# VectorE adds x for every group of the experts; layer norm of attended values on 33 rows a batch; eight unread products a batch

## The reference, cut to what matters

```python
# layer 3: of the 512 tokens of a batch 32 are chosen by score, the others get -1e9
scores = jnp.full_like(scores, -1000000000.0).at[b_idx, topk_idx].set(topk_vals)
return jax.nn.sigmoid(scores)         # their gate is 0, and all of them have one attended row
...
x = x + _layernorm(_L1_attn_ref(_layernorm(x, axis=-1), ...), axis=-1)

# layer 4: a causal attention, and then 8 experts, 2 of them chosen for a token
for e in range(N_EXPERTS):
    out = out + comb[:, e, None] * (t @ expert_w[e].T)
...
out = h + _moe(_rmsnorm(h, ffn_norm_w), gate_w, expert_w)
...
x = x + _layernorm(_L1_ffn_ref(_layernorm(x, axis=-1), ...), axis=-1)

def _layernorm(x, axis=-1, eps=1e-05):
    m = jnp.mean(x, axis=axis, keepdims=True)
    v = jnp.var(x, axis=axis, keepdims=True)
    return (x - m) / jnp.sqrt(v + eps)
```

## Time and profile before

| | us |
|---|---|
| median of 3 runs | 673.86 (671.64 to 676.05) |
| profiled execution, time | 673.91 |
| profiled execution, span | 672.2 |
| busy: PE / DVE / ACT / POOL | 552.9 / 505.7 / 360.5 / 269.6 |
| mean granted clock of PE | 0.848 of full |

### The profile page before, as it was taken

One profiled execution on the slowest core, in us unless ns is written; L12 is line 12 of the kernel. 1 busy time (PEld: TensorE's weight loads), 2 busy tenths in 40 slices (PEclk: granted clock), 3 DMA queues, 4 the chain that ended last, 5 costly groups with the idle time before them and its releaser, 6 DMA issues. The chain is left out here.

```text
span 672.2 us, 11846 instructions
## 1 busy us (share of the span) xinstructions
PE 552.9 (82%) x3809; PEld 313.0 (47%) x3809; DVE 505.7 (75%) x2306; ACT 360.5 (54%) x738; POOL 269.6 (40%) x501
## 2 busy tenths in 40 slices
PE   1875567988867999777999999999999898999870
PEld 1875467986656666311233333333333455465330
DVE  6599999454383778788899999999998056379784
ACT  5841134610200567501588788788878765466762
POOL 2001007721002476700354454545455454366784
PEclk9986675557967789855599999999999898999996
DMA  8000000210000066310011111111210000000001
GB/s 316 2 1 1 0 1 32 78 42 8 1 1 1 10 200 203 118 59 7 0 43 52 40 31 36 37 32 38 58 39 1 7 1 1 2 0 16 33 16 62
DMA packets 18876, 27.33 MB, mean 41 GB/s; under 512 B 3230, under 2 KB 14126, under 8 KB 18638
## 3 DMA queue, kind: packets, MB, share of 16 engines
q1 hardware_dynamic: 18174, 24.34, 11.6%
q10 hardware_dynamic: 576, 2.10, 0.9%
q0 software_dynamic: 64, 0.13, 0.1%
HBM read 14.11 MB, written 12.45 MB: 40 GB/s over the span
## 5 line engine op out<-in xcount | busy, mean ns | idle before, releaser
L904 DVE CUSTOM_DVE_ANT_0 w_qkvT<-d_pS,w_qkvT 128x512 bf16<-128x512 f32 x480 | 203.9, 485 | 17.3 <-PE d_pS L895 12.5
L1576 ACT ACTIVATE d_P<-pT 128x768 f32<-128x768 f32 (+1 forms) x192 | 165.9, 882 | 63.7 <-PE pT L1602 62.2
L1456 POOL TENSOR_SCALAR_AFFINE_SELECT d_P<-d_P 128x256 f32<-128x256 f32 x256 | 102.7, 415 | 134.7 <-ACT d_P L1576 134.7
L895 PE MATMUL d_pS<-Ks,Qs 48*128 48x512 bf16 x480 | 98.0, 325 | 13.3 <-DVE hadamard L904 8.9
L1602 PE MATMUL d_pO<-d_P,V 128*32 128x512 f32 (+3 forms) x1024 | 99.3, 463 | 1.4 <-POOL d_P L1456 0.9
L1602 PE MATMUL pT<-Qs,Ks 51*128 51x512 bf16 (+3 forms) x512 | 72.6, 311 | 1.9 <-ACT d_mT L1546 1.9
L895 PEld LDWEIGHTS d_pS<-Ks,Qs 48*128 48x128 bf16 x480 | 32.2, 96 | 56.7 <-DVE hadamard L904 52.0
L1602 PEld LDWEIGHTS pT<-Qs,Ks 51*128 51x128 bf16 x512 | 20.7, 94 | 73.8 <-ACT d_P L1576 42.8
L904 DVE DVE_READ_ACCUMULATOR2_ANT hadamard<- 128x1 f32 x512 | 42.5, 83 | 0.0
L1602 PEld LDWEIGHTS d_pO<-d_P,V 128*32 128x32 f32 x1024 | 21.3, 110 | 32.5 <-issue 29.6
L446 POOL MEMSET a_expS<- 1x1024 f32 x4 | 3.8, 945 | 78.7 <-DVE a_q L257 78.7
(11 more groups left out here) (314 smaller groups left out, 1073.1 us busy)
## 6 DMA issues: line engine op xcount, KB each, us to landing
Qs<-q_stack SPq DMA_DIRECT2D x32, 192.0 KB, 3.0
q_stack<-Qp SPq DMA_DIRECT2D x8, 384.0 KB, 2.5
X<-in_x_dram ACTq DMA_DIRECT2D x4, 512.0 KB, 6.2
n_rows<-N SPq DMA_DIRECT2D x4, 512.0 KB, 2.8
q_stack<-Qp SPq DMA_DIRECT2D x8, 256.0 KB, 2.5
out_dram<-e_moe SPq DMA_DIRECT2D x8, 256.0 KB, 2.0
w_qkvT<-in_w_qkvT_dram SPq DMA_DIRECT2D x1, 1536.0 KB
Ks<-k_stack SPq DMA_DIRECT2D x32, 48.0 KB, 3.2
```

Of the source, the lines that this page charges most:

```text
L895: last = nc.tensor.matmul(dst[:, at:at + w], top.Qs[c][rows, h % 8, 128 * q:128 * q + 128], top.Ks[c][rows, h // 4 % 2, 0:w], start=True, ...
L904: last = nc.vector.tensor_tensor_reduce(out=junk[:, at:at + w], in0=src[:, at:at + w], in1=top.wide_mask[:, 512 - w:512], scale=1.0, scala ...
L1456: last = nc.gpsimd.affine_select(out=view, in_=view, compare_op=ALU.is_ge, fill=0.0, base=0, pattern=[[0, 2], [1, 128]], channel_multiplie ...
L1576: nc.scalar.activation(P[pair % 4][:, :, P_AT[unit]:P_AT[unit] + w], pT[(3 * pair + unit) % 2][:, :, 0:w], ACT.Exp, scale=float(HD4) ** -0 ...
```

## The change

Projections: the norm of the attended values is taken ahead of the turns, on the rows themselves: for each half of the batches (Q), the 32 full rows a batch and the shared row, `Y + yU` and `yU`, get moments, a root, and are normalised; `Y` becomes the difference of the two normalised rows. PE's `attended` waits for them (`y_rows`), and DVE then adds `PY` to X for all four tiles in one instruction. The moments of `PY`, their root, and the step that kept the mean in `top.shift` are gone. The normalisation for N4 moves from POOL to DVE, in the turn after; the second part of K moves from ACT to POOL. DVE's wait for the memsets stands at the first copy to V4. Of ten unread products a batch eight are left.

Experts: x is added by DVE for every group (`add_x`, turn 12 + 4g), POOL's `finish` is gone; `scalars` stands ahead of `total` on DVE; the roots of the last two groups (ROOT_FROM), not only the last, are taken by ACT and DVE.

```diff
@@ projection_phase, POOL
+                def other_parts(n):
+                    pool.wait_ge(sm["kr"], n + 1)
+                    nc.gpsimd.tensor_copy(Kp[n % 3][:, 1, :], Kr[n % 2][:, :]).then_inc(sm["k2"], 1)
...
                 for turn in TURNS:
                     if turn - 2 in batches:
-                        third_parts(turn - 2)
-                    if turn - 1 in batches:
-                        normed(turn - 1)
+                        other_parts(turn - 2)
@@ projection_phase, DVE
+                def row_moments(Q):
+                    nc.vector.tensor_tensor(Y_full[Q][:, :], top.Y[Q][:, :], top.yU[Q][:, :], ALU.add)\
+                        .then_inc(sm["y_full"], 1)
+                    dve.wait_ge(sm["y_full"], Q + 1)
+                    nc.vector.bn_stats(y_st[Q][:, 0, :], Y_full[Q][:, :])
+                    nc.vector.bn_stats(y_st[Q][:, 1, :], top.yU[Q][:, :]).then_inc(sm["y_stats"], 1)
+                    dve.wait_ge(sm["y_stats"], Q + 1)
+                    for j in two:
+                        last = nc.vector.bn_aggr(y_mv[Q][:, j, :], y_st[Q][:, j, :])
+                    last.then_inc(sm["y_mv"], 1)
+                def normalise_rows(Q):
+                    dve.wait_ge(sm["y_std"], Q + 1)
+                    nc.vector.reciprocal(y_rs[Q][:, :], y_std[Q][:, :]).then_inc(sm["y_rstd"], 1)
+                    dve.wait_ge(sm["y_rstd"], Q + 1)
+                    for j, row in enumerate((Y_full[Q], top.yU[Q])):
+                        last = nc.vector.tensor_scalar(row[:, :], row[:, :], y_mv[Q][:, j, 0:1], y_rs[Q][:, j:j + 1],
+                                                       ALU.subtract, ALU.mult)
+                    last.then_inc(sm["y_norm"], 1)
+                    dve.wait_ge(sm["y_norm"], Q + 1)
+                    nc.vector.tensor_tensor(top.Y[Q][:, :], Y_full[Q][:, :], top.yU[Q][:, :], ALU.subtract)\
+                        .then_inc(sm["y_rows"], 1)
+                def attended(n):
+                    dve.wait_ge(sm["y_psum"], n + 1)
+                    nc.vector.tensor_tensor(X[:, R * n:R * n + R, :], PY[n % 2][:, :, :], X[:, R * n:R * n + R, :],
+                                            ALU.add).then_inc(sm["x"], 1)
+                def normed(n):
+                    dve.wait_ge(sm["norm"], n + 1)
+                    for t in range(R):
+                        last = nc.vector.tensor_scalar(N4[:, R * n + t, :], X[:, R * n + t, :], x_mv[n][:, t, 0:1],
+                                                       rs[n][:, 0, t:t + 1], ALU.subtract, ALU.mult)
+                    last.then_inc(sm["n4"], 1)
...
-                dve.wait_ge(sm["zeroed"], 2)
+                for Q in two:
+                    row_moments(Q)
+                for Q in two:
+                    normalise_rows(Q)
...
                 for turn in TURNS:
-                    if turn in batches:
-                        dve.wait_ge(sm["y_psum"], turn + 1)
-                        stats(lambda t: PY[turn % 2][:, t, :], y_st, y_mv, turn, "y_")
                     if turn - 2 in batches:
                         values(turn - 2)
                     if turn in batches:
                         attended(turn)
-                        dve.wait_ge(sm["x"], turn + 1)
-                        stats(lambda t: X[:, R * turn + t, :], x_st, x_mv, turn, "x_")
-                        shifts(turn)
+                        moments(turn)
+                    if turn - 1 in batches:
+                        normed(turn - 1)
+                    if turn in batches:
                         norm_scalars(turn)
@@ projection_phase, ACT, ahead of the turns
+                nc.scalar.activation(nb[0][:, 0:1], top.eps[:, :], ACT.Sqrt)
+                for Q in two:
+                    deviation_rows(Q)
@@ projection_phase, PE
                 def attended(n):
+                    pe.wait_ge(sm["y_rows"], n // 4 + 1)
                     wait(pe, sm["x"], n - 1)
...
                         keep_busy(turn - 1, 4)
                         by_channel(turn - 1)
-                        keep_busy(turn - 1, 6)
+                        keep_busy(turn - 1, 4)
                         project(turn - 1)
@@ experts_phase
+        ROOT_FROM = LAST - 1
-        GROUP_TURNS = {"total": 5, "deviation": 7, "scalars": 9, "normalise": 11, "finish": 13}
+        GROUP_TURNS = {"total": 5, "deviation": 7, "scalars": 9, "normalise": 11, "add_x": 12}
@@ experts_phase, POOL
                     for g in group_due(u, "deviation"):
-                        if g < LAST:
+                        if g < ROOT_FROM:
                             deviation(g)
-                    for g in group_due(u, "finish"):
-                        if g < LAST:
-                            finish(g)
@@ experts_phase, DVE
-                    for g in group_due(u, "total"):
-                        total(g)
+                    for g in group_due(u, "add_x"):
+                        if g < LAST:
+                            add_x(g)
                     for g in group_due(u, "scalars"):
                         scalars(g)
                         if g == LAST:
-                            dve.wait_ge(sm["out"], LAST)
                             finish_last()
+                    for g in group_due(u, "total"):
+                        total(g)
```

More of the change, by code:

```diff
@@ L925, in projection_phase @@
         ph = Phase(nc, ctx, "c_")
-        sm = ph.sems("rms_bias y_psum y_stats y_mv y_std y_rstd x y_shift shift x_stats x_mv std rstd norm a n4 aT_psum aT "
+        sm = ph.sems("rms_bias y_full y_stats y_mv y_std y_rstd y_norm y_rows y_psum x x_stats x_mv std rstd norm a n4 aT_psum aT "
                      "q_psum k_psum v_psum q1 k1 qr kr q2 k2 q3 k3 v_ready zeroed ones")
@@ L935, in projection_phase @@
         small = lambda name, *shape: [ph.sb(f"{name}{n}", [128, *shape]) for n in batches]
-        y_st, x_st, y_mv, x_mv = small("y_st", R, 6), small("x_st", R, 6), small("y_mv", R, 2), small("x_mv", R, 2)
-        y_std, y_rs, y_sh, nb = (small(name, R) for name in ("y_std", "y_rs", "y_sh", "nb"))
+        x_st, x_mv, nb = small("x_st", R, 6), small("x_mv", R, 2), small("nb", R)
+        Y_full = [ph.sb(f"Y_full{Q}", [128, D]) for Q in two]
+        y_st, y_mv = [ph.sb(f"y_st{Q}", [128, 2, 6]) for Q in two], [ph.sb(f"y_mv{Q}", [128, 2, 2]) for Q in two]
+        y_std, y_rs = [ph.sb(f"y_std{Q}", [128, 2]) for Q in two], [ph.sb(f"y_rs{Q}", [128, 2]) for Q in two]
         std, rs = small("std", 2, R), small("rs", 2, R)
@@ L1004, in stats, with moments @@
+                def attended(n):
+                    dve.wait_ge(sm["y_psum"], n + 1)
+                    nc.vector.tensor_tensor(X[:, R * n:R * n + R, :], PY[n % 2][:, :, :], X[:, R * n:R * n + R, :],
+                                            ALU.add).then_inc(sm["x"], 1)
+                def moments(n):
+                    dve.wait_ge(sm["x"], n + 1)
                     for t in range(R):
-                        last = nc.vector.bn_stats(st[n][:, t, :], src(t))
-                    last.then_inc(sm[s + "stats"], 1)
@@ L1007, in stats @@
-                    dve.wait_ge(sm[s + "stats"], n + 1)
+                        last = nc.vector.bn_stats(x_st[n][:, t, :], X[:, R * n + t, :])
+                    last.then_inc(sm["x_stats"], 1)
+                    dve.wait_ge(sm["x_stats"], n + 1)
                     for t in range(R):
[L1009 to L1016, removed]
-                    for t in range(R):
[L1018 to L1031, removed]
+                        last = nc.vector.bn_aggr(x_mv[n][:, t, :], x_st[n][:, t, :])
@@ L1033, in norm_scalars @@
+                    last.then_inc(sm["x_mv"], 1)
+                def normed(n):
+                    dve.wait_ge(sm["norm"], n + 1)
+                    for t in range(R):
+                        last = nc.vector.tensor_scalar(N4[:, R * n + t, :], X[:, R * n + t, :], x_mv[n][:, t, 0:1],
+                                                       rs[n][:, 0, t:t + 1], ALU.subtract, ALU.mult)
+                    last.then_inc(sm["n4"], 1)
                 def norm_scalars(n):
@@ L1120, in first_parts, with second_part @@
                         nc.scalar.activation(part[n % 3][:, 0, :], ps, ACT.Copy).then_inc(sm[s1], 1)
[L1122 to L1125, removed]
+                def second_part(n):
+                    act.wait_ge(sm["qr"], n + 1)
+                    nc.scalar.activation(Qp[n % 3][:, 1, :], Qr[n % 2][:, :], ACT.Copy).then_inc(sm["q2"], 1)
+                nc.scalar.activation(nb[0][:, 0:1], top.eps[:, :], ACT.Sqrt)
+                for Q in two:
+                    deviation_rows(Q)
                 act.wait_ge(sm["rms_bias"], 1)
@@ L1130, in _ @@
                         normalise(turn - 1)
-                    if turn in batches:
-                        deviation_y(turn)
                     if turn - 2 in batches:
-                        second_parts(turn - 2)
+                        second_part(turn - 2)
```

(10 more changed lines are left out.)

18 lines of the change are left out of this document (9 added, 9 removed).

## The result

| | before | after |
|---|---|---|
| median, same chip, 10 runs each | 671.88 us | 668.66 us (666.2 to 672.78) |
| ratio | | 0.9943, 95% 0.9918 to 0.9967 |
| profiled execution, time / span | 673.91 / 672.2 | 668.42 / 666.7 |
| busy: PE / DVE / ACT / POOL | 552.9 / 505.7 / 360.5 / 269.6 | 548.5 / 506.7 / 354.3 / 241.8 |

A forecast was written before the change was run, and what follows sets the result against it. Neither changed stage was one engine's alone: PE owns a projection turn, a chain of waits the experts' end. 673.91 - 5.0 (experts) - 2.2 (projections) = 666.7 us; own range 664.5 to 669, widened to 663 to 671.

The forecast's parts named there:

- The end of the experts: From the last scaled tile to the last addition: GpSimd's last sum sooner, total(7) unstretched, scalars earlier; -4.2 us.
- rival 1: Experts: each new addition costs VectorE's or GpSimd's next step 0.5 us, stretched steps stay; gain 1 or 2, total 670.2; 12%.
- The body of the experts: Experts before the end: additions on the path +1.4, stretched steps -1.8, scalars ahead of total -0.4; together -0.8 us.
- -1.8 of stretched steps: Experts' body: small VectorE steps stretched while GpSimd worked become short again; -1.8 us, -0.9 for the range.
- The turns: Projections: PE owns a turn, so two fewer unread products save 0.36 us in each of six turns; -2.2 us.
- rival 5: Projections give nothing, since ScalarE's copy, only 0.02 us behind, takes the dropped products' place; 668.9 us; 8%.
- The start: Start of projections: PE waits for normalised rows, but its filled idle gap pays for the delay; 0, at most +0.5 us.
- Rival 2: Start of projections: GpSimd's memsets hold up VectorE's row work, rows late by up to 2.1 us; 668.8 us; 8%.
- Rival 3: Start of projections: PE works without a gap and the clock rises before the third set; -2.8, 663.9 us; 10%.
- The tail: Seventh projection turn: ScalarE's copy 0.9 us sooner, given back by batch 7's normalisation ahead of the row maxima; sum 0.
- Rival 4: Projections: eight unread products are too few to hold the clock, turns take 12 to 13 us; 681 to 684 us; 4%.
- a sign that the ground is wrong: Causal attention, which nothing touches, moving by over 1 us would show the prediction wrong in its ground.

The follow-up runs named there:

- second profile: The kernel after, unchanged, run again beside the last experiments: ratio 0.9938, median 669.23 us.
- the old order: Kernel after with total again ahead of add_x and scalars on VectorE, and deviation ahead of normalise on ScalarE; additions and roots as after: ratio 0.9947.
- the fill held: Kernel after with GpSimd's memset of V4 held until VectorE has subtracted the rows: ratio 0.9901.

## Why the prediction was right in its range and half wrong in its sum

By its median, 668.66, the result lies in the range of 663 to 671, and also in the forecast's own 664.5 to 669. Part of that is luck: the kernel before ran at 671.88 beside it, not at the 673.86 that I started from. The ratio puts the gain at 0.57%, where 0.53 had been given to a gain of over 1% and 0.44 to one within. By the stages -4.2 (first profile) or -3.5 (second) was measured where the sum has -7.2:

- **The end of the experts**, forecast -4.2, measured -3.7: 6.94 from the last scaling, where 6.4 was forecast. The 0.5 that is missing is POOL's last sum, which I had done 1.65 after the last scaling; it was done after 2.13, since the sum before it took 1.06 beside the new addition. That is rival 1's mechanism, at 0.6 near its price of 0.5, in this one place on the path. The root's 1.3 is 1.4 in the end. The reason I put first was not the main one: `total(7)` did go from 1.73 to 0.69, but with the additions on POOL the end is only 0.3 longer. The order of the scalars does more (2.3 in the end, of which the body pays 0.8).
- **The body of the experts**, forecast -0.8, measured +0.35. Two terms failed, and by one cause. The -1.8 of stretched steps came to -0.2 (3.75 to 3.53), as rival 1 had it, and the -0.4 for the scalars ahead of `total` was a cost of 0.76 (77.56 with the old order). With the old order the small steps are 1.6 shorter than before, close to my 1.8, and the body is 0.41 shorter: the new order put them beside POOL's tile sums. The +1.4 for the additions is not shown by itself: moving them from POOL to DVE in the kernel after gives -0.22 in the body, where 1.4 - 1.8 would be -0.4.
- **The turns**, forecast -2.2 with one fall of the clock left. At full clock a turn went from 7.27 to 6.94, so six are 2.0 shorter. Two products were costed at 0.36 and gave 0.33; rival 5's floor lies right behind, from eight to six. The rest is the clock, and neither profile of after has a fall in the turns. The first has T0 to T6 3.8 shorter than before, which had one; the second 2.26 shorter, since its clock rose later after T0. That this is near -2.2 is luck.
- **The start**, forecast 0, measured +0.64. Rival 2 came true: PE could start at 213.58 where 211.4 was forecast, and 1.75 of that is the memset's. But three sets back to back took 9.16 us (213.58 to 222.74), where I had counted 3.71 for each, and that paid for most. The first transposes came at 224.15, between the forecast's 223.4 and rival 2's 225. With the fill held the start is 1.1 better than before. Rival 3's rise of the clock did not come.
- **The tail**, forecast 0, measured +2.3 and, in the second profile, +1.4. Here is the largest mis-sized term: ACT's sooner copy did give its 0.9 (T6 to the first maximum 5.83 before, 4.93 with the normalisation away), but the normalisation cost 2.44, not 0.96. I took the earlier trace rows, which stand beside no arithmetic of POOL, for a place beside POOL's third parts. By it the last projection starts 1.2 to 1.3 later after T6 than before. The first profile's other 0.9 is the clock: the last projection ran wholly at half of it, 5.40 us instead of 4.49 before and 4.62 in the second. What stays open: with the normalisation behind the eighth maximum the tail is no shorter (29.92), so a place where it would cost nothing was not found.
- **Rival 4** has its price (12 us without products), but eight were enough, and in this run's sample six.

The clock in the two profiles of after, first and second, for 8 us from about T0 on and then around the last projection (columns as in the earlier trace rows; the share ahead of the DMA columns is the granted clock):

```profile
224.00:232.00 8.00, 8.00 (x43) 5.13 (x43) 4.03 (x15) 4.20 (x10) 2.71 (x3) 0.90 0.00 0
226.00:234.00 8.00, 8.00 (x32) 4.12 (x31) 2.24 (x6) 3.38 (x9) 1.65 (x2) 0.67 0.00 0
```
```profile
274.00:281.00 7.00, 6.85 (x18) 2.92 (x18) 1.71 (x9) 1.18 (x2) 0.00 (x0) 0.50 0.35 115
278.00:285.00 7.00, 6.11 (x19) 2.21 (x18) 2.71 (x14) 1.18 (x2) 0.00 (x0) 0.68 0.33 107
```

The profiles of before and after differ by 5.5, of which 1.5 are the causal stage. I had called that a sign that the ground is wrong; it was not, since the same instructions took 283.46 and 284.50 in two profiles of the kernel after.

## What to carry to other kernels

Price an instruction that you move by what runs beside it at its new place, not by the row where it ran alone: here a `tensor_scalar` or an SBUF-to-SBUF copy on VectorE lasted as long as the memset beside it, and a two-input addition made GpSimd's sum beside it longer, on which VectorE then waited. A new order moves small steps to new neighbours too. Where several edits meet in one waiting chain, undo them one at a time before you name the cause, and compare stage by stage, since an untouched stage moved by up to 4.5 us between executions.

## What the runs showed of the hardware

- A VectorE `tensor_scalar` of 128x128 float32 took 2.29 us beside a GpSimd memset of 2.66, and 0.34 alone; a bfloat16 copy 2.65 and 0.13; a two-input addition beside a memset 0.29, as alone.
- Four `tensor_scalar` of 128x128 took 1.11 us beside an idle GpSimd, 1.38 in the turns, 2.52 and 3.14 beside two and three instructions of GpSimd.
- Two-input additions go both ways: a VectorE addition of 128x512 took 1.74 beside GpSimd's own of the same size and 0.68 beside a GpSimd addition of 128x128, which then took 1.06 instead of 0.46. A VectorE step of 128x4 took 0.72 beside a GpSimd addition of 128x256 and 0.16 alone.
- The clock can stand at its lower level with PE busy for 93% of 40 us (0.65 and 0.58 granted, without the unread products), while turns with them held 1.00.
- The untouched causal stage took 280.9 us at a mean granted clock of 0.928 and 285.3 at 0.912.
